# Zero matmuls ahead of the first weights, and the values of a batch weighed in one step: a two-layer decoder on one core

## The reference

```python
def _L0_attn_ref(x, Wq, bq, Wk, bk, Wv, bv, Wo, bo):
    B, L, D, H = (32, 64, 512, 32)
    HD = D // H
    b, l, d = x.shape
    h, hd = (H, HD)
    q = (x @ Wq.T + bq).reshape(b, l, h, hd).transpose(0, 2, 1, 3)
    k = (x @ Wk.T + bk).reshape(b, l, h, hd).transpose(0, 2, 1, 3)
    v = (x @ Wv.T + bv).reshape(b, l, h, hd).transpose(0, 2, 1, 3)
    scores = jnp.einsum('bhqd,bhkd->bhqk', q, k) / math.sqrt(hd)
    causal = jnp.tril(jnp.ones((l, l), bool))
    scores = jnp.where(causal, scores, -jnp.inf)
    att = jax.nn.softmax(scores, axis=-1)
    out = jnp.einsum('bhqk,bhkd->bhqd', att, v)
    out = out.transpose(0, 2, 1, 3).reshape(b, l, d)
    return out @ Wo.T + bo
```

## Time and profile before

| what | us |
|---|---|
| median of the runs (850.72 to 855.27) | 851.04 |
| the profiled execution | 849.07 |
| its span, first to last instruction | 847.3 |
| TensorE busy (share of the span) | 812.5 (96%) |
| VectorE busy | 574.4 (68%) |
| ScalarE busy | 432.6 (51%) |

### The profile page before, as it was taken

The page is one execution under the profiler, slowest core; times in us unless marked ns, Lnnn a source line. Parts: engine busy times, 40 slices in busy tenths (PEclk is TensorE's granted clock), DMA queues, the critical chain, the costliest instruction groups (busy, mean ns, idle before and its releaser), DMA issues.

```text
span 847.3 us, 22622 instructions
## 1 busy us (share of the span) xinstructions
PE 812.5 (96%) x9288; PEld 673.8 (80%) x9288; DVE 574.4 (68%) x1510; ACT 432.6 (51%) x1109; POOL 262.2 (31%) x310
## 2 busy tenths in 40 slices
PE   6999999999999999999998999999999999999996
PEld 6888887675557787777776789988989899989993
DVE  5675666586876666677776547983767566756776
ACT  4454444568763343465555446634644475347532
POOL 0221522579976532112222567710000100010001
PEclk9999999999999999999999999999999999999999
DMA  8410002222221200010000122320000010000001
GB/s 306 142 53 16 16 22 83 66 70 56 72 63 38 63 22 9 20 29 18 19 19 19 32 62 89 100 65 26 1 2 2 1 50 2 2 1 27 2 2 50
DMA packets 20998, 36.77 MB, mean 43 GB/s; under 512 B 3200, under 2 KB 7424, under 8 KB 20640
## 3 DMA queue, kind: packets, MB, share of 16 engines
q1 hardware_dynamic: 20800, 35.20, 13.6%
q10 hardware_dynamic: 96, 0.13, 0.1%
HBM read 30.86 MB, written 2.10 MB: 39 GB/s over the span
## 4 chain that ended last, share of the span: by engine, by line
PE 78%; DVE 10%; ACT 4%; issue 2%; POOL 2%; DMA 2%; SPq 1%; ACTq 0%; POOLq 0%; DVEq 0%
PE bank L833 18%; PE bank L835 16%; PE bank L834 16%; PE bank L984 6%; PE bank L1259 5%; PE bank L1004 2%; PE bank L1121 2%; DVE tank L2565 2%; PE bank L989 2%; DVE tank L2345 1%; PE bank L954 1%; PE bank L1108 1%; PE bank L1243 1%; DMA x_all<-x_dram 1%; PE bank L1278 1%
## 5 line engine op out<-in xcount | busy, mean ns | idle before, releaser
L833 PE MATMUL bank<-wr,hTl 128*128 128x512 f32 (+3 forms) x392 | 153.5, 391 | 1.3 <-issue 0.8
L835 PE MATMUL bank<-wr,hTh 128*128 128x512 f32 (+3 forms) x392 | 147.0, 375 | 0.0
L834 PE MATMUL bank<-wr,hTh 128*128 128x512 f32 (+3 forms) x392 | 146.6, 374 | 0.0
L1562 ACT ACTIVATE pT<-bank 128x512 f32<-128x512 f32 x128 | 70.0, 605 | 94.9 <-PE bank L954 94.9
L2345 DVE TENSOR_REDUCE tank<-bank 128x4 f32<-128x512 f32 x128 | 82.0, 682 | 42.4 <-PE bank L954 42.4
L833 PEld LDWEIGHTS bank<-wr,hTl 128*128 128x128 f32 (+1 forms) x392 | 73.7, 188 | 17.7 <-issue 5.3
L835 PEld LDWEIGHTS bank<-wr,hTh 128*128 128x128 f32 (+1 forms) x392 | 73.7, 188 | 12.6
L834 PEld LDWEIGHTS bank<-wr,hTh 128*128 128x128 f32 (+1 forms) x392 | 73.8, 188 | 11.3 <-issue 1.0
L833 PE MATMUL bank<-hTh,wr 128*128 128x256 f32 (+1 forms) x272 | 82.0, 302 | 0.0
L834 PE MATMUL bank<-hTl,wr 128*128 128x256 f32 (+1 forms) x272 | 81.3, 299 | 0.0
L835 PE MATMUL bank<-hTh,wr 128*128 128x256 f32 (+1 forms) x272 | 81.2, 298 | 0.0
(11 more groups left out here) (257 smaller groups left out, 1923.8 us busy)
## 6 DMA issues: line engine op xcount, KB each, us to landing
raw<-w_qkv_dram SPq DMA_DIRECT2D x12, 256.0 KB, 2.8
raw<-w_xq_dram SPq DMA_DIRECT2D x16, 192.0 KB, 2.3
raw<-w_xo_dram SPq DMA_DIRECT2D x12, 256.0 KB, 2.8
cin<-xT_dram SPq DMA_DIRECT2D x8, 256.0 KB, 3.6
x_all<-x_dram SPq DMA_DIRECT2D x8, 256.0 KB, 7.0
cin<-ctx_dram SPq DMA_DIRECT2D x8, 256.0 KB, 3.4
cin<-ctxT_dram SPq DMA_DIRECT2D x8, 256.0 KB, 2.9
out_dram<-x_all SPq DMA_DIRECT2D x8, 256.0 KB, 2.0
```

The lines of the kernel that those rows point to most:

```text
L833: mm(dst, lhs[1], rhs[0], start=start, stop=False)
L834: mm(dst, lhs[0], rhs[1], start=False, stop=False)
L835: return mm(dst, lhs[0], rhs[0], start=False, stop=stop)
L1562: av(pT[e][:, 2 * rows + n, :], t_bank[n][:, :], ACT.Exp).then_inc(exp_ready, 1)
```

## The change

It has two parts. GpSimd fills a tile with zeros first, and TensorE multiplies it with itself 17 times, 512 columns each, ahead of `first_pair`; the results are overwritten. In both self attentions the two parities of a batch are weighed one behind the other at r = 1, where parity 1 was weighed before; parity 0 leaves r = 3 of the step before last. The drain is changed in the same way.

```diff
+        idle = nc.alloc_sbuf_tensor_at("idle", [P, P], BF16, offset=ARENA + 4 * SPARE)
...
+        CLOCKED = 17
...
+            def keep_clocked():
+
+                pe.wait_ge(idle_ready, 1)
+                for _ in range(CLOCKED):
+                    mm(t_bank[0][:, :], idle[:, :], idle[:, :].unsqueeze(1).broadcast_to([P, KT, P]), start=True, stop=True, skip_group_check=True)
...
@@ -1028,9 +1037,8 @@
                     maxima_turned(l, of_step(l, i, "max"))
                 scores(l, i)
                 if r == 1 and 0 <= b - 2 < B:
-                    weigh_values(l, b - 2, 1)
-                if r == 3 and 0 <= b - 1 < B:
-                    weigh_values(l, b - 1, 0)
+                    for e in range(2):
+                        weigh_values(l, b - 2, e)
...
+            keep_clocked()
             first_pair()
...
             scores(0, DRAIN + 1)
-            weigh_values(0, B - 2, 1)
+            for e in range(2):
+                weigh_values(0, B - 2, e)
             x_spectrum(1)
...
             scores(1, DRAIN + 1)
-            weigh_values(1, B - 2, 1)
+            for e in range(2):
+                weigh_values(1, B - 2, e)
             attention_out(1, B - 3)
...
         def _(pool):
+            nc.gpsimd.memset(idle[:, :], 0.0).then_inc(idle_ready, 1)
```

More of the change, by code:

```diff
@@ L320, in decoder @@
         consts_ready = sem("consts_ready")
+        idle_ready = sem("idle_ready")
         w0_hi = sem("w0_hi")
```

## The result

The changed kernel takes 866.2 us in the median (866.02 to 866.45, 4 runs), the kernel before 852.63 us in the runs made with it. The ratio is 1.0165, with a 95% interval of 1.0142 to 1.0188. The direction of the forecast was right; the size was not. It started from 851.04 us, the median of three runs before; with the fourth that median is 852.63 us, and put on top of it the forecast's 8.7 us would still leave 4.9 us unexplained.

The account below looks back on a forecast made before the run. TensorE was taken to bound the kernel except where it waits, with the additional rows' chain binding five second-layer batches. Zeros 0, first layer +2.4, second +6.3: +8.7 us on 851.04 gives 859.7 us, 1.0% slower; range 855.0 to 861.8 us.

Parts of the forecast that it names:

- I take 0: Start of kernel: zeros gain 0, since the next matmul still starts at 20.31 us; TensorE's wait grows from 0.76 to 2.4 us.
- the bound of -1.6 us: Start of kernel: the zeros' best case, the clock rises earlier and all of the 1.6 us saved in `first_pair` passes through.
- The price of weighing: Both self attentions: one call takes 1.01 us, two behind each other 1.88 us; 14 changed batches shrink TensorE's work by 2.0 us.
- They start about 1.0 us later: Step r = 1: exponentials writing `pT[0]` wait for parity 0's weighing; first-layer cost +1.0 at i = 25, +0.97 at 29 and 33.
- The fixed chain in the second layer: S(3) to S(6): turned rows of k come 0.87 us later, then a fixed 10.5 to 11.0 us; 4 x 0.87 = +3.5 us.
- S(7) +0.97 us: Second layer, S(7): ScalarE has exponentials, half of q and all of k in a row, costing +0.97 us.

Follow-up runs that it names:

- the gaps filled: Changed kernel plus 4 useless 512-column matmuls at i = 27 and i = 31 of each layer, where parity 0 was weighed before: 861.56 us, ratio 1.0108 to the kernel before.
- five batches in pairs: Changed kernel, zeros kept, with batches 5 and 6 of each layer weighed as before, only 0 to 4 in pairs: 854.72 us, ratio 1.0025 to the kernel before.
- the two queues: Kernel before, with ScalarE issuing 4 of the 8 additional-row DMAs for every second-layer batch, not only two: 849.61 us against 853.08 us, ratio 0.9955.
- the pairs alone: Kernel before with the edits to `weigh_values` but without the zeros: 869.69 us, ratio 1.0206 to the kernel before.

## Why the prediction was right in its terms and wrong in its sum

- **The zeros, "I take 0": mis-sized.** The term followed the one trace, and for that execution it was right: the next matmul started at 20.01 us in place of 20.31 us, because the DMA of `x_all` landed 0.3 us earlier; the wait was 1.50 us and not 2.4, since the first weights came at 7.37 us. But TensorE's margin of 0.76 us is smaller than what the landing of the first weights (6.86, 7.41, 8.00, 8.50 us in four traces) and the moment of the rise vary by. Measured, the zeros are worth 1.7 us alone, near the bound of -1.6 us. What the traces show of it is less: in the five without zeros TensorE is 0 to 1.1 us behind VectorE's chain at the start, 0.5 us in the mean. The rest of the 1.7 us is not explained. This error made the sum too high, and so hid a part of the one below.
- **The price of weighing: right.** Pairs take 1.88 us in the trace after.
- **"They start about 1.0 us later" at i = 25, 29 and 33: right.** TensorE's wait of 0.48 us for `pT` at 150.29 us is the one that the forecast named; those of 0.48 us at 132.42 us and of 1.24 us at 167.80 us come from the same delay. With the gaps filled, the turned maxima at i = 32 are 0.9 us (first layer) and 2.8 us (second) behind the kernel with only five batches in pairs, against 0.97 and 2.9 us forecast for the sums that end there.
- **The fixed chain in the second layer, +3.5 us and S(7) +0.97 us: right**: with five batches in pairs 4.5 us were measured against 4.45, and the two queues show that the chain sets the pace.
## What to carry to other kernels

Work that a wait hides is not free to remove: on TensorE it can also hold the clock, so price an emptied gap once more with the work that follows it at half speed, not only by what starts next. When something moves within a cycle that is bound by a chain, ask on which side of the chain's first instruction it lands: in front of the turned rows it cost 0.87 us per batch, behind them it was free for the chain (but not for the readers of its own result). And a margin read from one trace is worth no more than its spread: take a second trace of the start before calling an edit hidden.

## What the runs showed of the hardware that I had not expected

- The granted clock went to 0.50 after rests of 1.39 us plus 0.81 to 0.92 us, and also behind a single rest of 1.39 us at the start of a drain. Work that had already begun again was hit by it. In the changed kernel the low stretches lasted 3.4 us in the first layer and 6.8 us in the second; with the pairs alone they were 3.4, 6.8, 3.4 and 10.2 us. Rests of 1.39 us (i = 7, and ahead of 200.35 us) and one of 2.87 us in the cross attention left it at 1.00.
- 16 useless matmuls in the four gaps made the program 4.6 us faster.
- The granted clock that the views give for 7 to 10 us of the kernel before is 1.00, while its matmuls stand 0.22 us apart, twice the distance of later ones: at the very start of an execution only the distances tell the level.
- Moving half of 8 small DMA issues (0.6 us each) to a second engine's queue for five more batches took 3.8 us off the program, 2.8 us of it within the second self attention.
